# Three of eight contraction tiles of layer 2 as fp32r products of halves, in a four-layer kernel on one core

## The chip, the cores and the metric

The kernel runs on one core of one Trainium2 chip. The metric is the device time of one execution in microseconds. Each core has five engines with an instruction queue each, which work off their queues in order and meet at semaphores: TensorE (PE, matrix products, with weight loads shown apart as PEld), VectorE (DVE), ScalarE (ACT), GpSimd (POOL) and SyncE (SP). Here SP issues the loads and stores, and GpSimd issues transfers that add to what lies in SBUF.

## The reference

Eight batches of 256 rows and 1024 columns in fp32 go through four layers, each with a residual:

```python
x = x + (x @ W0.T + (x @ A0[label]) @ B0.T * 0.5)           # layer 0, low rank 32
x = x + quantise(x, thresholds, deltas, zero_points)        # layer 1, eight groups
x = x + x @ W2[adapter].T                                   # layer 2, weights by batch
x = x + (x @ B3[adapter].T) @ A3[adapter].T                 # layer 3, rank 16
```

In layer 1 the group of an element is the number of thresholds that its magnitude does not exceed; it is rounded with the step and zero point of its group (the last group's for eight), clipped to levels 0 to 63 and scaled back, and is zero where it exceeds none of the thresholds. The kernel works out a candidate for each of the eight groups, and masks choose among them.

## The kernel before, in words

**Layout.** x is held transposed: 128 partitions by eight tiles of 256 rows each (2048 columns for a batch). Each matrix product has 128x128 weights and 128x256 data. An output tile `o` of layer 0 or 2 sums eight contraction tiles `k`.

**Layer 0** (`main0`, `close0`, in order by `tile0`) works with fp32r halves: w0 and x are split once into a high and a low half, and a product becomes three (high by high, high by low, low by high; L773). From batch 2 on the low half of x is made so: ACT copies x into `x_hi` (L369), writes its negative into `x_lo` (L374), and GpSimd issues a transfer that adds `x_raw` to it (L340). A low-rank part (L799, L806) closes each tile (L783).

**Layer 1** runs on ACT and DVE in units (`quantise(u)`): for batch 0 two halves, for batches 1 to 6 one unit of 2048 columns each, for batch 7 three pieces. For each of eight groups ACT makes a candidate (L439) and from the second on a mask (L449); DVE scales (L608), clips (L616) and merges (L628, L634). There are three candidate buffers and two masks, so candidate j+2 and test j+1 wait for merge j-1. At the end DVE adds the result to x2 (L685). `between(u, j)` puts the other work of ACT and DVE between the groups: ACT's splits and drains (`split_batch`, `split_a3`, `drain_low`, `drain_l0`, `drain_bx`, `split_bx`), and DVE's `drain_l2`, `split_a3`, `low_rank_lo` and `split_bx`. `drain_l0` (L400) moves a half of layer 0 from PSUM to x2; from batch 2 on it waits until x3 of the batch two before is complete, since that reads the same slot.

**Layer 2** (`layer2(b, q)`, L838) works in fp32, in four quarters of two output tiles. Two PSUM banks alternate, so quarter 2 waits for DVE's drain of quarter 0 (L595, `x3_done`) and quarter 3 for that of quarter 1. The weights come in 1 MB chunks of two tiles, three chunks deep (`w2_sb`). Batch 7 goes another way (`last_layer2`, L853), by parts of k.

**Layer 3** multiplies x3 with B3 (`low_rank3`, L872), has ACT copy it to `bx_parts` (L412), sums the pieces on PE (`sum_bx`, L879), splits (L421 on ACT, L587 on DVE), multiplies with A3 (L902) and has DVE add it (`finish`, L600); then SP stores.

**PE's order.** In step s = 1 to 6 PE does the four quarters of layer 2 of batch s-1, with the low-rank product and sum of batch s+2 before quarters 2 and 3, then seven tiles of layer 0 (`AHEAD`); behind the third of these comes `low_rank3` of batch s-1, behind the fourth `sum_bx`, behind the fifth layer 3. DVE and ACT work at the same time on unit s. The layer 0 tile with o = 0 needs the bank that ACT's `drain_l0` of the batch before has emptied. In step 1 that tile is the third of the seven, in step 2 the fourth.

## Time and profile before

| | us |
|---|---|
| median of 3 runs | 464.55 |
| lowest, highest | 464.13, 465.97 |
| the profiled execution | 464.56 |
| its span, first to last instruction | 462.7 |
| busy: PE, DVE, ACT, GpSimd | 454.7, 415.4, 326.7, 8.1 |

The span is 1.86 us shorter than the time of the same execution. Busy times are those of the whole span; they do not tell which engine sets the end of a step, since an engine can have idle time that lies in one place only. The granted clock of TensorE was 0.998 of full over the span.

### The profile page before, as it was taken

Reading aid. Unit: us, or ns where it says so; the run is one execution under the profiler, and the core shown is the slowest. Engines: PE = TensorE matmul, PEld = TensorE weight load, DVE = VectorE, ACT = ScalarE, POOL = GpSimd, SP = SyncE. Lnnn points to the kernel's source line nnn. Section 1 sums busy time; section 2 is a strip of 40 time slices with the busy share of each in tenths; the row PEclk is TensorE's granted clock in tenths of the full one; section 3 lists DMA queues with packets and bytes.
Section 4 is the critical chain, followed back from the end, with each engine's and each line's share of the span. In section 5 each row is a group of like instructions: output and inputs, shape, how many; then the busy total and the mean of one; then the engine's idle time right before and its main releaser. Section 6 shows DMA issues by size and latency. Waiting matters only on the chain.

```text
span 462.7 us, 7306 instructions
## 1 busy us (share of the span) xinstructions
PE 454.7 (98%) x3006; PEld 410.9 (89%) x3006; DVE 415.4 (90%) x395; ACT 326.7 (71%) x274; POOL 8.1 (2%) x18
## 2 busy tenths in 40 slices
PE   7999999999999999999999999999999999999995
PEld 7899999889998899889998899989998899988884
DVE  4889999999699996999699996999869999999983
ACT  5699979958398747967398754996349848665730
POOL 1000000000000000000000000100000000000000
PEclk9999999999999999999999999999999999999999
DMA  7983430557128534367227543183322522245242
GB/s 279 343 334 104 91 103 1 91 188 279 69 92 221 196 142 159 69 204 279 76 91 188 197 174 126 48 261 132 120 92 91 181 92 96 75 173 180 94 159 91
DMA packets 17941, 69.15 MB, mean 149 GB/s; under 512 B 2421, under 2 KB 3445, under 8 KB 13045
## 3 DMA queue, kind: packets, MB, share of 16 engines
q1 hardware_dynamic: 17044, 62.41, 37.5%
q0 software_dynamic: 864, 6.29, 7.3%
q8 instruction: 23, 0.38, 0.3%
q14 instruction: 10, 0.07, 0.1%
HBM read 54.01 MB, written 8.39 MB: 135 GB/s over the span
## 4 chain that ended last, share of the span: by engine, by line
PE 90%; DMA 3%; issue 2%; DVE 2%; SPq 2%; ACT 1%; DVEq 0%; ACTq 0%
PE l_ps L838 39%; PE l_ps L773 37%; PE l_ps L853 6%; PE bx_ps L872 2%; PE l_ps L783 2%; DMA w_sb<-w 2%; PE bx_ps L799 2%; DMA adapter_ids<-adapters 1%; PE l_ps L902 1%; PE bx_ps L806 1%; PE bx_ps L879 1%; DVE quant L628 1%; ACT cand L439 0%; ACT magnitude L429 0%; SPq L287 0%
## 5 line engine op out<-in xcount | busy, mean ns | idle before, releaser
L838 PE MATMUL l_ps<-x,w_sb 128*128 128x256 f32 x896 | 196.9, 380 | 0.4 <-DVE x L595 0.4
L838 PEld LDWEIGHTS l_ps<-x,w_sb 128*128 128x128 f32 x896 | 169.2, 190 | 25.3 <-issue 2.8
L634 DVE COPY_PREDICATED quant<-mask,cand 128x2048 f32<-128x2048 int8 (+2 forms) x77 | 145.6, 1891 | 0.4
L439 ACT ACTIVATE cand<-x,inv_delta 128x2048 f32<-128x2048 f32 (+2 forms) x88 | 134.5, 1528 | 8.8 <-DVE quant L628 7.0
L449 ACT ACTIVATE mask<-magnitude,thr_bias 128x2048 fp8e5<-128x2048 f32 (+2 forms) x77 | 117.7, 1529 | 13.4 <-DVE quant L634 12.7
L608 DVE TENSOR_SCALAR cand<-cand,delta 128x2048 f32<-128x2048 f32 (+2 forms) x88 | 87.9, 999 | 10.1 <-ACT cand L439 9.8
L616 DVE TENSOR_SCALAR cand<-cand,lower,upper 128x2048 f32<-128x2048 f32 (+2 forms) x88 | 93.4, 1062 | 0.4
L773 PE MATMUL l_ps<-x_hi,w_hi 128*128 128x256 f32 x512 | 87.1, 292 | 0.9 <-DVE x_lo L565 0.9
L773 PE MATMUL l_ps<-x_hi,w_lo 128*128 128x256 f32 x512 | 82.8, 283 | 0.0
L773 PE MATMUL l_ps<-x_lo,w_hi 128*128 128x256 f32 x512 | 82.5, 283 | 0.0
L773 PEld LDWEIGHTS l_ps<-x_hi,w_hi 128*128 128x128 f32 x512 | 71.4, 191 | 6.6 <-issue 4.2
L773 PEld LDWEIGHTS l_ps<-x_hi,w_lo 128*128 128x128 f32 x512 | 70.7, 192 | 0.2 <-DVE w_lo L559 0.2
L773 PEld LDWEIGHTS l_ps<-x_lo,w_hi 128*128 128x128 f32 x512 | 70.6, 191 | 0.0
L400 ACT ACTIVATE x<-l_ps 128x1024 f32<-128x1024 f32 x16 | 16.3, 1020 | 26.3 <-PE l_ps L783 18.1
L595 DVE TENSOR_TENSOR x<-l_ps,x 128x512 f32<-128x512 f32 x32 | 22.5, 704 | 3.4 <-PE l_ps L853 1.8
L853 PE MATMUL l_ps<-x,w_sb 128*128 128x256 f32 x96 | 21.6, 381 | 0.0
L421 ACT ACTIVATE bx_split<-bx_ps 128x256 fp32r<-128x256 f32 x8 | 3.1, 383 | 25.3 <-PE bx_ps L879 17.4
L853 PEld LDWEIGHTS l_ps<-x,w_sb 128*128 128x128 f32 x96 | 18.1, 190 | 2.9 <-issue 0.4
L628 DVE SCALAR_TENSOR_TENSOR quant<-magnitude,sorted_thr,cand 128x2048 f32<-128x2048 f32 (+2 forms) x11 | 19.4, 1764 | 0.0
L685 DVE TENSOR_TENSOR x<-x,quant 128x2048 f32<-128x2048 f32 (+2 forms) x11 | 18.8, 1708 | 0.1
L587 DVE SCALAR_TENSOR_TENSOR bx_split<-bx_split,not_bx_hi,bx_ps 128x256 fp32r<-128x256 f32 x8 | 3.8, 481 | 16.7 <-ACT bx_split L421 16.7
L600 DVE TENSOR_TENSOR x<-l_ps,x 128x512 f32<-128x512 f32 x24 | 15.1, 688 | 3.7 <-PE l_ps L902 3.1
(66 smaller groups left out, 231.0 us busy)
## 6 DMA issues: line engine op xcount, KB each, us to landing
w_sb<-w SPq DMA_DIRECT2D x31, 1024.0 KB, 4.9
out<-x SPq DMA_DIRECT2D x32, 256.0 KB, 2.2
x_raw<-x SPq DMA_DIRECT2D x15, 512.0 KB, 6.4
x_lo<-x_raw POOLq DMA_DIRECT2D x6, 1024.0 KB, 8.2
a_raw<-a SPq DMA_DIRECT2D x8, 512.0 KB, 3.6
w_sb<-w SPq DMA_DIRECT2D x7, 512.0 KB, 7.4
b_sb<-b SPq DMA_DIRECT2D x8, 256.0 KB, 2.7
a_raw<-a SPq DMA_DIRECT2D x8, 128.0 KB, 6.3
```

Of the source, the lines that this page charges most:

```text
L400: act.activation(x2[:, b % SLOTS, h * HW:(h + 1) * HW], l0_ps[:, h, :], ACT.Copy).then_inc(x0_done, 1)
L439: act.activation(cand[:, c % CANDS, 0:n], x2_unit(u), ACT.Identity, bias=ROUND, scale=inv_delta[:, k:k + 1]).then_inc(rounded, 1)
L449: act.activation(mask[:, m % MASKS, 0:n], magnitude[:, 0:n], ACT.Relu, bias=thr_bias[:, k:k + 1], scale=STEEP, saturate=False).then_inc(ma ...
L595: dve.tensor_tensor(x3[:, cols], l2_bank(b, q), x2[:, b % SLOTS, cols], ALU.add).then_inc(x3_done, 1)
L608: dve.tensor_scalar(t, t, -ROUND, delta[:, k:k + 1], ALU.add, ALU.mult).then_inc(scaled, 1)
L616: dve.tensor_scalar(t, t, lower[:, k:k + 1], upper[:, k:k + 1], ALU.max, ALU.min).then_inc(clipped, 1)
L628: dve.scalar_tensor_tensor(y, magnitude[:, 0:n], sorted_thr[:, G - 1:G], t, ALU.is_gt, ALU.mult)\
L634: dve.copy_predicated(y, mask[:, m % MASKS, 0:n].bitcast(I8), t).then_inc(merged, 1)
L685: dve.tensor_tensor(x2_unit(u), x2_unit(u), quant[:, 0:UNITS[u][2]], ALU.add).then_inc(x2_done, 1)
L773: nc.tensor.matmul(dst, w[:, o, k * P:(k + 1) * P], v[:, b % 2, k * S:(k + 1) * S], start=(o % 2 == 0 and v is x_hi and w is w0_hi and k = ...
L838: last = nc.tensor.matmul(l2_bank(b, q)[:, i * S:(i + 1) * S], w2_tile(b, o)[:, k * P:(k + 1) * P], x2[:, b % SLOTS, k * S:(k + 1) * S], s ...
L853: last = nc.tensor.matmul(l2_bank(b, q)[:, i * S:(i + 1) * S], w2_tile(b, o)[:, k * P:(k + 1) * P], x2[:, b % SLOTS, k * S:(k + 1) * S], s ...
```

## The change

For batches 0 to 6, contraction tiles 0 to 2 (`EDGE = 3`) of layer 2 are now computed like layer 0, as three fp32r products of halves; tiles 3 to 7 stay fp32. In each quarter the fp32 products of both output tiles come first, then the fp32r ones. Batch 7 stays fp32 throughout.

- **Weights.** Layer 2's weights are loaded tile by tile, in two parts: 640 columns into a ring of five (`w2_sb`), and 384 columns, the "edge", into a ring of three (`w2_edge`). ACT copies an edge to `w2_hi` and writes its negative to `w2_lo` (rings of four), and GpSimd issues a transfer that adds the edge to `w2_lo`.
- **x2.** ACT copies the first 768 columns of x2 of the finished batch to `x2_hi`, and DVE subtracts to get `x2_lo`.
- **Room.** To fit into SBUF, w0 is staged in the candidate buffers, `a3_raw` lies in the second half of x3 (so it is loaded behind the stores), one `parts` serves for `low_parts` and `bx_parts`, B3 is held at half the width, and batch 7's last tiles go to freed buffers.

The core of the diff:

```diff
-CHUNKS = 3
+
+EDGE = 3
+SPLIT = B - 1
+EW = EDGE * P
+EX = EDGE * S
+
+RING = 5
+RAW = 3
+HALVES = 4
...
-        w2_sb = sb("w2_sb", [P, CHUNKS, 2, T * P], F32)
+        w2_sb = sb("w2_sb", [P, RING, T * P - EW], F32)
+        w2_edge = sb("w2_edge", [P, RAW, EW], F32)
+        w2_hi = sb("w2_hi", [P, HALVES, EW], F32R)
+        w2_lo = sb("w2_lo", [P, HALVES, EW], F32R)
+        x2_hi = sb("x2_hi", [P, EX], F32R)
+        x2_lo = sb("x2_lo", [P, EX], F32R)
...
+        def hi_tile(b, o):
+            return w2_hi[:, (T * b + o) % HALVES, :]
+
+        def lo_tile(b, o):
+            return w2_lo[:, (T * b + o) % HALVES, :]
+
+        def a3_raw(b):
+            return x3[:, HW:BW] if b < B - 1 else quant[:, HW:BW]
...
+            def load_w2(b, o, adapter):
+                n = T * b + o
+                if b == B - 1 and o >= RING:
+                    sp.wait_ge(x2_done, LAST)
+                elif n >= RING:
+                    sp.wait_ge(w2_used, n - RING + 1)
+                sp.dma_start(w2_tile(b, o), w2[bass.ds(adapter, 1), o, :, EW:T * P].rearrange("l p w -> p (l w)"))\
+                  .then_inc(w2_loaded[o] if b < B - 1 else last_w2_loaded[o], 16)
...
+                elif n >= RAW:
+                    sp.wait_ge(w2_added[(n - RAW) % T], 16 * ((n - RAW) // T + 1))
+                sp.dma_start(edge_tile(b, o), w2[bass.ds(adapter, 1), o, :, 0:EW].rearrange("l p w -> p (l w)"))\
+                  .then_inc(w2_edge_loaded[o] if b < B - 1 else last_w2_loaded[o], 16)
...
+            for o in range(RAW, T - 1):
+                load_edge(0, o, adapter)
+            for s in range(1, B):
...
+                for o in range(RING, T):
+                    load_w2(s - 1, o, adapter)
+                load_edge(s - 1, T - 1, adapter)
+                adapter = adapter_of(s)
+                if s < B - 1:
+                    for o in range(RING):
+                        load_w2(s, o, adapter)
+                        if o == 1 and s + 3 < B:
                             load_batch(s + 3)
-                    if s == B - 1:
-                        load_w2(s, 3, adapter)
-                    load_adapter(s, adapter)
-                for q in range(4) if s < B else LAST_ORDER:
+                        if o < RAW:
+                            load_edge(s, o, adapter)
+                    for o in range(RAW, T - 1):
+                        load_edge(s, o, adapter)
+                else:
+                    for o in range(RING):
+                        load_edge(s, o, adapter)
...
+                load_b3(s, adapter)
+                for q in range(4):
                     store(s - 1, q)
+                if s < B - 1:
+                    load_a3(s, adapter)
...
-            for b in range(ADDED, B):
-                add_x(b)
+            def add_w2(b, o):
+                pool.wait_ge(w2_neg_done, T * b + o + 1)
+                pool.dma_start(lo_tile(b, o), edge_tile(b, o), accum_op=ALU.add).then_inc(w2_added[o], 16)
+
+            add_x(2)
+            for o in range(HALVES):
+                add_w2(0, o)
+            for s in range(1, B):
+                if s + 2 < B:
+                    add_x(s + 2)
+                for o in range(HALVES, T):
+                    add_w2(s - 1, o)
+                if s < SPLIT:
+                    for o in range(HALVES):
+                        add_w2(s, o)
...
+            def split_w2(b, o):
+                n = T * b + o
+                act.wait_ge(w2_edge_loaded[o], (b + 1) * 16)
+                if n >= HALVES:
+                    act.wait_ge(l2_done, n - HALVES + 1)
+                act.activation(hi_tile(b, o), edge_tile(b, o), ACT.Copy).then_inc(w2_hi_done, 1)
+                act.wait_ge(w2_hi_done, n + 1)
+                act.activation(lo_tile(b, o), hi_tile(b, o).bitcast(F32), ACT.Copy, scale=-1.0).then_inc(w2_neg_done, 1)
+
+            def split_x2(b):
+                act.wait_ge(x2_done, x2_count(b))
+                if b > 0:
+                    act.wait_ge(l2_done, T * b)
+                act.activation(x2_hi[:, :], x2[:, b % SLOTS, 0:EX], ACT.Copy).then_inc(x2_hi_done, 1)
...
+                    if j >= 4:
+                        split_w2(0, j - 4)
                 elif s < B - 1:
-                    if j == 1 and s + 2 < B:
-                        split_batch(s + 2)
+                    if j == 1:
+                        split_x2(s - 1)
+                        if s + 2 < B:
+                            split_batch(s + 2)
+                    if j == 2:
+                        split_w2(s - 1, 4)
+                        split_w2(s - 1, 5)
                     if j == 3:
                         split_a3(s - 1)
                         if s + 2 < B:
                             drain_low(s + 2)
-                    if j == 4 and s + 2 < B:
-                        low_rank_hi(s + 2)
+                    if j == 4:
+                        split_w2(s - 1, 7)
+                        if s + 2 < B:
+                            low_rank_hi(s + 2)
+                    if j == 5 and s < SPLIT:
+                        split_w2(s, 0)
+                        split_w2(s, 1)
                     if j == 6:
                         drain_l0(s + 1, 0)
+                        if s < SPLIT:
+                            split_w2(s, 2)
+                            split_w2(s, 3)
...
                 elif u == LAST:
+                    if j == 1:
+                        split_x2(s - 1)
                     if j == 2:
                         split_a3(s - 1)
                     if j == 3:
                         drain_l0(s, 1)
+                    if j >= 4:
+                        split_w2(s - 1, j)
...
+                    if j == 4 and 0 < UNITS[u][0] < B - 1:
+
+                        split_w2(UNITS[u][0] - 1, 6)
...
+            def split_x2(b):
+                dve.wait_ge(x2_hi_done, b + 1)
+                dve.tensor_tensor(x2_lo[:, :], x2[:, b % SLOTS, 0:EX], x2_hi[:, :].bitcast(F32),
+                                  ALU.subtract).then_inc(x2_split_done, 1)
...
                     for q in range(4):
                         finish(UNITS[u][0] - 1, q)
+                if UNITS[u][0] < SPLIT and u > 0:
+                    split_x2(UNITS[u][0])
...
             def layer2(b, q):
-                pe.wait_ge(w2_loaded[q], (b + 1) * 16)
                 if q == 0:
                     pe.wait_ge(x2_done, x2_count(b))
                     if b > 0:
                         pe.wait_ge(out_done, 4 * b - 1)
-                else:
-                    if q > 1:
-                        pe.wait_ge(x3_done, b * 4 + q - 1)
+                elif q > 1:
+                    pe.wait_ge(x3_done, b * 4 + q - 1)
+
                 for i in range(2):
                     o = 2 * q + i
-                    for k in range(T):
-                        last = nc.tensor.matmul(l2_bank(b, q)[:, i * S:(i + 1) * S], w2_tile(b, o)[:, k * P:(k + 1) * P],
-                                                x2[:, b % SLOTS, k * S:(k + 1) * S], start=(k == 0), stop=(k == T - 1))
-                last.then_inc(l2_done, 1)
+                    pe.wait_ge(w2_loaded[o], (b + 1) * 16)
+                    for k in range(EDGE, T):
+                        last = nc.tensor.matmul(l2_bank(b, q)[:, i * S:(i + 1) * S], w2_block(b, o, k),
+                                                x2[:, b % SLOTS, k * S:(k + 1) * S], start=(i == 0 and k == EDGE),
+                                                stop=False)
+                    last.then_inc(w2_used, 1)
+                if q == 0:
+                    pe.wait_ge(x2_split_done, b + 1)
+                for i in range(2):
+                    o = 2 * q + i
+                    pe.wait_ge(w2_added[o], 16 * (b + 1))
+                    hi = hi_tile(b, o)
+                    lo = lo_tile(b, o)
+                    for w, v in ((hi, x2_hi), (hi, x2_lo), (lo, x2_hi)):
+                        for k in range(EDGE):
+                            last = nc.tensor.matmul(l2_bank(b, q)[:, i * S:(i + 1) * S], w[:, k * P:(k + 1) * P],
+                                                    v[:, k * S:(k + 1) * S], start=False,
+                                                    stop=(i == 1 and w is lo and k == EDGE - 1))
+                    last.then_inc(l2_done, 1)
```

**How the order moves.** The names are those of the tiles without their numbers: `x<-l_ps` on ACT is `drain_l0`, `w_hi<-w_edge` with `w_lo<-w_hi` a `split_w2`, `x_hi<-x` of 128x768 ACT's `split_x2`. Line numbers of the changed kernel differ from those of the kernel before.

DVE, from the last merge of unit 1 to the first merge of unit 2. Before:

```order
L634 COPY_PREDICATED quant<-mask,cand 128x2048 [waits merged,masked,clipped]
L587 SCALAR_TENSOR_TENSOR bx_split<-bx_split,not_bx_hi,bx_ps 128x256 [waits bx_hi_done]
L685 TENSOR_TENSOR x<-x,quant 128x2048 [waits merged]
L600 TENSOR_TENSOR x<-l_ps,x 128x512 [waits l3_done] x3
L600 TENSOR_TENSOR x<-bx_ps,x 128x512 [waits l3_done]
L608 TENSOR_SCALAR cand<-cand,delta 128x2048 [waits rounded]
```

Now:

```order
L781 COPY_PREDICATED quant<-mask,cand 128x2048 [waits merged,masked,clipped]
L729 SCALAR_TENSOR_TENSOR bx_split<-bx_split,marks,bx_ps 128x256 [waits bx_hi_done]
L832 TENSOR_TENSOR x<-x,quant 128x2048 [waits merged]
L742 TENSOR_TENSOR x<-l_ps,x 128x512 [waits l3_done] x3
L742 TENSOR_TENSOR x<-bx_ps,x 128x512 [waits l3_done]
L746 TENSOR_TENSOR x_lo<-x,x_hi 128x768 [waits x2_hi_done]
L755 TENSOR_SCALAR cand<-cand,delta 128x2048 [waits rounded]
```

The subtraction for `x2_lo` of the finished batch now stands between the finishes and the first scaling of the next unit, with a wait for ACT.

ACT, from the split of `bx` at the end of a unit to the split of the next x. Before:

```order
L421 ACTIVATE bx_split<-bx_ps 128x256 [waits l3_done,bx_sum_done]
L400 ACTIVATE x<-l_ps 128x1024 [waits x3_done,l0_done]
L439 ACTIVATE cand<-x,inv_delta 128x2048 [waits merged,x0_done]
L429 ACTIVATE magnitude<-x 128x2048 [waits masked,merged,x0_done]
L439 ACTIVATE cand<-x,inv_delta 128x2048 [waits merged]
L449 ACTIVATE mask<-magnitude,thr_bias 128x2048 [waits merged,mag_done]
L439 ACTIVATE cand<-x,inv_delta 128x2048 [waits merged]
L369 ACTIVATE x_hi<-x_raw 128x1024 [waits l0_done,x_loaded0]
```

Now:

```order
L524 ACTIVATE bx_split<-bx_ps 128x256 [waits l3_done,bx_sum_done]
L502 ACTIVATE x<-l_ps 128x1024 [waits x3_done,l0_done]
L559 ACTIVATE cand<-x,inv_delta 128x2048 [waits merged,x0_done]
L547 ACTIVATE magnitude<-x 128x2048 [waits masked,merged,x0_done]
L559 ACTIVATE cand<-x,inv_delta 128x2048 [waits merged]
L569 ACTIVATE mask<-magnitude,thr_bias 128x2048 [waits merged,mag_done]
L559 ACTIVATE cand<-x,inv_delta 128x2048 [waits merged]
L539 ACTIVATE x_hi<-x 128x768 [waits l2_done,x2_done]
L467 ACTIVATE x_hi<-x_raw 128x1024 [waits l0_done,x_loaded0]
```

The copy to `x2_hi` stands behind three candidates' worth of work of the next unit: candidates 0 to 2, the magnitude and test 1.

ACT, from candidate 7 to the split of `bx`. Before:

```order
L439 ACTIVATE cand<-x,inv_delta 128x2048 [waits merged]
L400 ACTIVATE x<-l_ps 128x1024 [waits x3_done,l0_done]
L449 ACTIVATE mask<-magnitude,thr_bias 128x2048 [waits merged]
L412 ACTIVATE bx_parts<-bx_ps 128x256 [waits bx_sum_done,bx_done]
L421 ACTIVATE bx_split<-bx_ps 128x256 [waits l3_done,bx_sum_done]
```

Now:

```order
L559 ACTIVATE cand<-x,inv_delta 128x2048 [waits merged]
L502 ACTIVATE x<-l_ps 128x1024 [waits x3_done,l0_done]
L531 ACTIVATE w_hi<-w_edge 128x384 [waits l2_done,w2_edge_loaded2]
L533 ACTIVATE w_lo<-w_hi 128x384 [waits w2_hi_done]
L531 ACTIVATE w_hi<-w_edge 128x384 [waits l2_done,w2_edge_loaded3]
L533 ACTIVATE w_lo<-w_hi 128x384 [waits w2_hi_done]
L569 ACTIVATE mask<-magnitude,thr_bias 128x2048 [waits merged]
L515 ACTIVATE parts<-bx_ps 128x256 [waits bx_sum_done,low_sum_done,bx_done]
L524 ACTIVATE bx_split<-bx_ps 128x256 [waits l3_done,bx_sum_done]
```

Four instructions, two weight pairs, now stand between the drain of layer 0, which waits for x3, and the drain of `bx`, for which PE waits.

## Rows read from the trace of the kernel before

**Rows 1.** The page: busy us, share of the span, instructions.

```profile
PE 454.7 (98%) x3006; PEld 410.9 (89%) x3006; DVE 415.4 (90%) x395; ACT 326.7 (71%) x274; POOL 8.1 (2%) x18
```

**Rows 2.** Waits of PE: line waited for, us in total, times, longest.

```profile
PE l_ps L910 <- POOL ident L323: 1.5, 1, 1.5
```

**Rows 3.** Windows, step 2: length, then busy us by engine, clock, DMA share.

```profile
133.60:186.30 52.70, 52.70 (x349) 47.44 (x348) 48.42 (x37) 38.53 (x28) 0.86 (x1) 1.00 0.50 157
```

**Rows 4.** Chain in order of time, step 2: start us, us, what.

```profile
155.97 6.91 PE l_ps L838 x32
162.88 2.87 PE l_ps L773 x24
...
176.05 0.43 PE bx_ps L879 x2
...
186.32 13.82 PE l_ps L838 x64
```

**Rows 5.** DVE's timeline, steps 1 and 2: start, us, instruction [idle before].

```profile
129.63 1.28 DVE L608 TENSOR_SCALAR cand<-cand,delta 128x2048 f32<-128x2048 f32 x1
...
133.40 2.35 DVE L628 SCALAR_TENSOR_TENSOR quant<-magnitude,sorted_thr,cand 128x2048 f32<-128x2048 f32 x1
...
143.51 2.52 DVE L634 COPY_PREDICATED quant<-mask,cand 128x2048 f32<-128x2048 int8 x1
...
147.54 0.69 DVE L595 TENSOR_TENSOR x<-l_ps,x 128x512 f32<-128x512 f32 x1 [0.28 <-PE l_ps L838]
...
165.21 0.69 DVE L595 TENSOR_TENSOR x<-l_ps,x 128x512 f32<-128x512 f32 x1
...
182.34 1.28 DVE L608 TENSOR_SCALAR cand<-cand,delta 128x2048 f32<-128x2048 f32 x1
```

**Rows 6.** ACT's timeline, step 2.

```profile
166.00 1.03 ACT L400 ACTIVATE x<-l_ps 128x1024 f32<-128x1024 f32 x1 [2.02 <-DVE x L595]
...
176.52 0.39 ACT L421 ACTIVATE bx_split<-bx_ps 128x256 fp32r<-128x256 f32 x1 [3.20 <-PE bx_ps L879]
...
187.25 1.99 ACT L369 ACTIVATE x_hi<-x_raw 128x1024 fp32r<-128x1024 f32 x2
```

**Rows 7.** Groups by form: busy, mean ns; neighbours of the new forms.

```profile
L369 ACT ACTIVATE x_hi<-x_raw 128x1024 fp32r<-128x1024 f32 x14 | 14.0, 1044 | 0.0
...
L421 ACT ACTIVATE bx_split<-bx_ps 128x256 fp32r<-128x256 f32 x8 | 3.1, 383 | 25.3 <-PE bx_ps L879 17.4 <-PE bx_ps L872 7.8
...
L565 DVE TENSOR_TENSOR x_lo<-x_raw,x_hi 128x512 fp32r<-128x512 f32 x4 | 2.8, 688 | 3.9 <-ACT x_hi L362 3.9
...
L362 ACT ACTIVATE x_hi<-x_raw 128x512 fp32r<-128x512 f32 x4 | 2.4, 622 | 3.4 <-DMA x_raw<-x 3.4
L571 DVE TENSOR_TENSOR x_lo<-x_raw,x_hi 128x1024 fp32r<-128x1024 f32 x2 | 2.4, 1232 | 0.0
```

**Rows 8.** DMA issues: KB each, median us to landing.

```profile
out<-x SPq DMA_DIRECT2D x32, 256.0 KB, 2.2
...
x_lo<-x_raw POOLq DMA_DIRECT2D x6, 1024.0 KB, 8.2
```

**Rows 9.** ACT's timeline, step 1.

```profile
81.50 1.99 ACT L369 ACTIVATE x_hi<-x_raw 128x1024 fp32r<-128x1024 f32 x2
```

**Rows 10.** Waits of ACT from 239.00 to 291.70 us.

```profile
ACT x L400 <- PE l_ps L783: 2.6, 1, 2.6
```

**Rows 11.** ACT's timeline, unit 6.

```profile
341.48 1.02 ACT L400 ACTIVATE x<-l_ps 128x1024 f32<-128x1024 f32 x1 [6.46 <-PE l_ps L783]
...
351.93 1.99 ACT L449 ACTIVATE mask<-magnitude,thr_bias 128x2048 fp8e5<-128x2048 f32 x1
```

**Rows 12.** DVE's timeline: first merge of unit 6, last x2 addition.

```profile
349.47 2.34 DVE L628 SCALAR_TENSOR_TENSOR quant<-magnitude,sorted_thr,cand 128x2048 f32<-128x2048 f32 x1
...
444.38 0.68 DVE L685 TENSOR_TENSOR x<-x,quant 128x512 f32<-128x512 f32 x1
```

**Rows 13.** PE's timeline: its last part of layer 2.

```profile
446.73 5.45 PE L853 MATMUL l_ps<-x,w_sb 128*128 128x256 f32 x24
```

## What I predict

> **What bounds the kernel now.** First the page: TensorE (PE) is busy 98% of the span [rows 1]. Then the waits with PE as the waiting engine: the longest is 1.5 us, before its first product, and no other of the four lines reaches 1 us [rows 2]. Then one steady step in the windows: in 52.70 us PE is busy 52.70, VectorE (DVE) 48.42, ScalarE (ACT) 38.53, at the full granted clock [rows 3]. So PE is the bound, but DVE has only 4.3 us of slack in a step. The chain in order of time shows PE's step as a grid [rows 4]: a quarter of layer 2 takes 6.91 us, a tile of layer 0 (24 fp32r products and a short one) 3.00 us.
>
> The reader should then put DVE's and ACT's timelines of this step beside the grid [rows 5, 6]. ACT reaches batch s-1's `bx` work early, waits for PE's sum (ends 176.48), splits `bx`, drains layer 0, and only then starts the candidates of the next batch. DVE, its merges done, waits there too, then adds (L685), finishes (L600) and opens the next batch's unit with L608 at 182.34, 5.86 us after PE's sum.
>
> **The change part by part.**
>
> PE: a fp32 product takes 13.82 us / 32 = 0.432 us, a fp32r one 2.87 us / 24 = 0.120 us [rows 4]. Three of the latter save 0.072 us; 3 x 8 x 7 = 168 of them save **12.1 us**, 1.73 us in a step. The page shows no cost for changing between the kinds: a layer 0 tile behind layer 2 takes 2.87 us. The Trainium skill (FP8 and Floating Point Precision, TensorE Precision Notes) says that true fp32 makes four passes. As an estimate from that page, at one pass for fp32r, three products would cost three quarters of one, and 168 x 0.108 = 18.1 us would be saved; the row says 0.83 of one, and the row decides.
>
> DVE: one subtraction of 128x768 (`x2_lo`) for each of seven batches. Its neighbours are 0.688 us (128x512) and 1.232 us (128x1024) [rows 7]; I take 0.95. With it DVE has 49.4 us of work in a step.
>
> ACT: a conversion of 128x768 per batch (between 0.622 and 1.044 us [rows 7], taken as 0.83), and for each of 56 weight tiles a copy and a negation of 128x384, of which the second waits for the first. One lies between 0.383 and 0.622 us [rows 7]; a pair is bounded by 0.8 and 1.3, taken as 1.02. In a step 8 x 1.02 + 0.83 = 9.0 us on top of 38.53: 47.5 us, which fits by itself. ACT's waits in the step are 14 us.
>
> GpSimd and the queues: 56 adding transfers of 192 KB. The nearest rows are the 1 MB adding transfer (8.2 us to landing) and the 256 KB store (2.2 us) [rows 8]; I take 4.5, nearer to the store by size but with descriptors from GpSimd. The Trainium skill (DMA: Bandwidth & Descriptors, Anatomy of one DMA — SWDGE (gpsimd) path) gives 2.0 us plus bytes over 436 GB/s: an estimate of 2.5 us here, and 4.4 for the 1 MB one, where the trace has 8.2. By either figure up to 5.0 us the sum below is the same. On SP the stores of batch s-1 now stand behind `edge` loads that wait for these adds, but the last of those adds lands by the end of the unit, before the first store may go; `a3`, loaded behind the stores, has ten microseconds in hand. I cost these at nothing; w2's tiles are asked for a quarter or more ahead.
>
> **What is not hidden is the order.** DVE's new subtraction of batch b stands before the first L608 of unit b+1, and waits for `x2_hi`, which ACT makes only after five full operations of unit b+1. Before, ACT's same place is the first L369, at 187.25: 10.77 us behind PE's sum at 176.48 [rows 4, 6]. So with t for the end of PE's sum and d for the time at which DVE may start a unit: d = t + 10.77 + 0.83 + 0.95 = **t + 12.55**, where it was t + 5.86. DVE starts each unit 6.7 us later against PE, more than its slack. What is late next, from offsets in the same unit (start 129.63; merge 2 at 143.51) [rows 5]:
> - x3's quarter 3 is ready at d + 36.0 (165.21 + 0.69 is 36.3, less a wait of 0.28 at 147.54). ACT's drain of layer 0 waits for that; behind it in ACT's queue now stand two weight pairs, a test and the `bx` drain that PE's sum needs: 0.1 + 0.95 + 2.05 + 1.9 + 0.45, and the sum itself with its signals 0.5: **t' = d + 42.0**.
> - Tile 7's low half: merge 2 ends at d + 16.4; a test, a pair, a candidate and a pair on ACT give d + 22.3; with 4.5 for the add, 1.08 of products and 13.60 to the sum: d + 41.5.
> So a step is 42.0 + 12.55 = 54.55 us instead of 52.70; PE's gain of 1.73 us turns into waits.
>
> Now step by step, t before being 123.78, 176.48, 229.19, 281.89, 334.60 (176.48 from [rows 4]; the others are the same sum in the other steps):
> - Start: ACT's first full unit reaches L369 at 81.50 [rows 9]. Four weight pairs stand before it; the first fits into a wait of ACT for PE, three delay it by 3.1. d = 81.5 + 3.1 + 0.83 + 0.95 = 86.4.
> - Step 1: here the layer 0 tile that needs the drained bank stands before the low-rank work of batch 0. x3 complete 86.4 + 36.0, bank free 1.1 later, then 3.00 + 1.00 + 3.18 + 0.43 on PE and 0.1 of signals: t = 131.2 (+7.4).
> - Steps 2 to 4: 54.55 each: 185.8, 240.3, 294.9.
> - Step 5: ACT's second drain of layer 0 waits 2.6 us for PE [rows 10]. Before, this went into slack; now it moves d: t = 352.0 (+17.4).
> - Unit 6 depends on PE's last tile of batch 6: ACT's drain starts 6.88 us behind the sum (341.48) and the place of `x2_hi` comes 10.45 us later (351.93) [rows 11]: d = 352.0 + 6.88 + 10.45 + 0.83 + 0.95 = 371.1. Before, DVE's first merge of this unit began at 349.47 [rows 12]; less 3.77 (129.63 to 133.40 [rows 5]) that is a start at 345.7. DVE is 25.4 us late.
> - From there to its last x2 addition (ends 445.07 [rows 12]) DVE had hardly a gap; one more subtraction adds 0.95. PE then began its last part at 446.73, 1.66 behind [rows 13]. The end moves by 25.4 + 0.95 - 1.66 = 24.7 us. PE's own path (last layer 2 of the steps from 423, then 48.9 us) comes out level with this, at 472.
> The profiled execution took 464.56 us, 1.86 over its span and equal to the median of 464.55. **Forecast: 464.6 + 24.7 = 489 us**.
>
> **The rivals.**
> 1. PE stays the bound: 464.6 - 12.1 = **452.5 us**. (By the Trainium skill's estimate of 18.1 us, FP8 and Floating Point Precision again, this would be 446.5.) This needs `x2_hi` to be done when DVE finishes, at t + 5.9, so ACT would have to be 5.7 us further ahead. ACT's idle time in the step speaks for it; that the idle time lies before the `bx` work and not behind it [rows 6] speaks against it. It decides for the faster side only if that order is not as I read it.
> 2. The adding transfers are slow: at the 8.2 us of [rows 8] tile 7 sets t' = d + 45.2, 3.2 us more in four steps and 0.4 in the first: **502 us**. It decides from a landing of 5.0 us. For it: ten times as many of them, beside more and smaller loads; against it: a fifth of the size.
> 3. Milder: ACT's weight pairs hide and a step stays at about 52.7, the start and unit 6 remaining: 7.4 less in four steps, **482 us**; with half of the start hidden too, 478.
> 4. The gain and the late start cancel (within 0.5% of 464.6): it would take a shift of 6.7 us that costs just 12 us over the kernel; nothing in the rows points there.
>
> **How the numbers follow.** My forecast 0.60, rival 2 0.16, rival 3 0.14, rival 1 0.06, rival 4 0.04. The pair's bounds (0.8 to 1.3) move the forecast by -2 to +2.5 us, the 128x768 forms by 1.3 either way; so its own range is 484 to 494. The range goes down to rival 3's lower figure with its own margin and up past rival 2: 476 to 508. A measurement of this kernel tells about 0.5% from no change: faster 0.06, same 0.04, slower 0.90.
>
> **What would show it.** DVE's largest wait would be its `x2_lo` subtraction (L746) for ACT's `x2_hi` (L539), 4.6 us in the middle steps, more at both ends, some 40 us in all. A step from one layer 2 to the next would be near 54.5 us; a quarter of layer 2 without waits 6.48 us. PE's busy share would fall to some 91%, with new waits for x3 (L737), for ACT's drain and for its `parts`; ACT's L502 would wait for L737. Wrong would be: steps of 51 us, or L539 done before L742; a long wait of L1000 for the adds would mean rival 2.

## The result: slower by 7.4%

| | before | after |
|---|---|---|
| median, us | 464.54 | 499.02 |
| lowest, highest | 463.6, 466.0 | 497.43, 500.81 |
| profiled execution, its span | 464.56, 462.7 | 500.81, 499.0 |
| busy PE, DVE, ACT, GpSimd | 454.7, 415.4, 326.7, 8.1 | 452.9, 420.9, 384.6, 71.7 |

The ratio is 1.0737 (95% interval 1.0686 to 1.0788): 34.5 us more. The forecast was 489.0 us with a range from 476 to 508 and a chance of 0.90 for slower. The direction and the range held; the size was 10 us short.

The page of the changed kernel answers to [rows 1]; then the shares of the chain by engine, and the landing of the new adds, beside [rows 8]. The chain is the path of work that ended last, followed back from each wait to what released it (L429 adds, L746 is `x2_lo`, L539 `x2_hi`, L531 and L533 the weight pair):

```profile
PE 452.9 (91%) x3174; PEld 413.4 (83%) x3174; DVE 420.9 (84%) x402; ACT 384.6 (77%) x393; POOL 71.7 (14%) x74
...
PE 40%; DVE 19%; issue 15%; ACT 13%; DMA 10%; SPq 2%; DVEq 0%; ACTq 0%
...
w_lo<-w_edge POOLq DMA_DIRECT2D x56, 192.0 KB, 4.1
```

PE has not become the one engine of the chain again: its busy time is nearly what it was and its share has fallen to 91%, as forecast. It fell by only 1.8 us instead of 12.1; some 7 us of the missing 10.3 are products that ran at a lower granted clock (last section), the rest isn't placed. The waits that answer to [rows 2] (engine, line, what it waited for; total us, times, longest):

```profile
PE l_ps L1000 <- DMA w_lo<-w_edge: 13.8, 7, 2.9
PE l_ps L987 <- DVE x L737: 12.4, 6, 3.0
PE l_ps L1000 <- DVE x_lo L746: 7.3, 3, 5.0
...
DVE x_lo L746 <- ACT x_hi L539: 43.8, 6, 11.6
...
ACT x L502 <- DVE x L737: 10.7, 5, 4.0
```

DVE waits 43.8 us for `x2_hi`; before, it had no such operation. The chain of step 2 answers to [rows 4] (start, us, what):

```profile
132.15 0.45 PE bx_ps L1042 x2
...
143.44 0.74 ACT x_hi L539
...
144.21 0.96 DVE x_lo L746
...
161.64 1.89 issue
163.53 0.52 ACT w_hi L531
164.06 0.53 ACT w_lo L533
...
164.99 5.95 DMA w_lo<-w_edge
...
170.98 2.41 PE l_ps L1000 x18
...
186.56 0.63 PE bx_ps L1042 x2
```

From PE's sum the chain goes to ACT, which reaches `x2_hi` after 10.8 us; then DVE subtracts and opens its unit at 145.16; from DVE's third merge it goes over a test and a weight pair of ACT, an adding transfer of 5.95 us, 18 products and four tiles of layer 0 (with `low_rank3` before the last) to the end of the next sum, at 187.19. A step is 54.6 us here.

### The profile page after: what moved, and what is told of

Its sections match the earlier page's. It is cut to its first block, busy times and chain, and to the rows that moved or that the text cites. A ratio compares the mean times of both kernels' runs of the same rounds, so it can differ in the third digit from the quotient of the medians.

```text
span 499.0 us, 8182 instructions
## 1 busy us (share of the span) xinstructions
PE 452.9 (91%) x3174; PEld 413.4 (83%) x3174; DVE 420.9 (84%) x402; ACT 384.6 (77%) x393; POOL 71.7 (14%) x74
## 4 chain that ended last, share of the span: by engine, by line
PE 40%; DVE 19%; issue 15%; ACT 13%; DMA 10%; SPq 2%; DVEq 0%; ACTq 0%
PE l_ps L922 25%; DVE cand L755 7%; DMA w_lo<-w_edge 6%; PE l_ps L1016 5%; DVE quant L781 5%; ACT cand L559 4%; ACT mask L569 3%; PE l_ps L1000 3%; DVE quant L775 3%; PE l_ps L987 3%; ACT magnitude L547 2%; DMA cand<-w 2%; PE bx_ps L1035 2%; DMA w_sb<-w 2%; DVE x L737 1%
## 5 line engine op out<-in xcount | busy, mean ns | idle before, releaser
L987 PE MATMUL l_ps<-x,w_sb 128*128 128x256 f32 x560 | 126.7, 381 | 12.4 <-DVE x L737 12.4
L987 PEld LDWEIGHTS l_ps<-x,w_sb 128*128 128x128 f32 x560 | 105.2, 191 | 28.6 <-DVE x L737 15.0
L429 POOL DMA_DIRECT2D w_lo<-w_edge x56 | 64.7, 1168 | 240.3 <-ACT w_lo L533 239.0
L922 PE MATMUL l_ps<-x_hi,w_hi 128*128 128x256 f32 x512 | 87.2, 292 | 3.8 <-ACT x L502 2.4
L922 PE MATMUL l_ps<-x_hi,w_lo 128*128 128x256 f32 x512 | 83.7, 286 | 0.0
L922 PE MATMUL l_ps<-x_lo,w_hi 128*128 128x256 f32 x512 | 83.5, 285 | 0.0
L922 PEld LDWEIGHTS l_ps<-x_hi,w_hi 128*128 128x128 f32 x512 | 72.1, 194 | 9.6 <-issue 3.7
L922 PEld LDWEIGHTS l_ps<-x_lo,w_hi 128*128 128x128 f32 x512 | 71.7, 194 | 0.0
L1000 PE MATMUL l_ps<-x_hi,w_hi 128*128 128x256 f32 x168 | 35.3, 320 | 21.1 <-DMA w_lo<-w_edge 13.8
L1000 PEld LDWEIGHTS l_ps<-x_hi,w_hi 128*128 128x128 f32 x168 | 26.2, 197 | 26.1 <-DMA w_lo<-w_edge 16.5
L746 DVE TENSOR_TENSOR x_lo<-x,x_hi 128x768 fp32r<-128x768 f32 x7 | 6.7, 959 | 43.8 <-ACT x_hi L539 43.8
L502 ACT ACTIVATE x<-l_ps 128x1024 f32<-128x1024 f32 x16 | 16.3, 1018 | 27.7 <-PE l_ps L932 17.0
L531 ACT ACTIVATE w_hi<-w_edge 128x384 fp32r<-128x384 f32 x56 | 28.6, 510 | 8.8 <-DMA w_edge<-w 8.8
L533 ACT ACTIVATE w_lo<-w_hi 128x384 fp32r<-128x384 f32 x56 | 29.4, 525 | 1.8
L1000 PE MATMUL l_ps<-x_hi,w_lo 128*128 128x256 f32 x168 | 30.5, 292 | 0.0
L1000 PE MATMUL l_ps<-x_lo,w_hi 128*128 128x256 f32 x168 | 30.4, 292 | 0.0
```

The source lines that it names most:

```text
L429: pool.dma_start(lo_tile(b, o), edge_tile(b, o), accum_op=ALU.add).then_inc(w2_added[o], 16)
L531: act.activation(hi_tile(b, o), edge_tile(b, o), ACT.Copy).then_inc(w2_hi_done, 1)
L533: act.activation(lo_tile(b, o), hi_tile(b, o).bitcast(F32), ACT.Copy, scale=-1.0).then_inc(w2_neg_done, 1)
L922: nc.tensor.matmul(dst, w[:, o, k * P:(k + 1) * P], v[:, b % 2, k * S:(k + 1) * S], start=(o % 2 == 0 and v is x_hi and w is w0_hi and k = ...
L987: last = nc.tensor.matmul(l2_bank(b, q)[:, i * S:(i + 1) * S], w2_block(b, o, k), x2[:, b % SLOTS, k * S:(k + 1) * S], start=(i == 0 and k ...
L1000: last = nc.tensor.matmul(l2_bank(b, q)[:, i * S:(i + 1) * S], w[:, k * P:(k + 1) * P], v[:, k * S:(k + 1) * S], start=False, stop=(i == 1 ...
```

## Experiments

Each ratio is to runs of the kernel before taken beside it. The theory after the result was this: one loop holds the step, PE's sum, ACT's `x2_hi`, DVE's unit, and back to the sum. The rivals were that the adding transfers, or ACT's and PE's own added work, do it.

### x2_hi early

```diff
                 candidate(u, 0)
+                if 0 < UNITS[u][0] and UNITS[u][1] == 0:
+                    split_x2(UNITS[u][0] - 1)
                 take_magnitude(u)
...
                     if j == 1:
-                        split_x2(s - 1)
```

> The changed kernel with one edit: ACT makes x2_hi of the finished batch right behind candidate 0 of the next unit, not behind candidate 2. Theory A (the place of x2_hi in ACT's queue holds DVE up, by 43.8 us in all): x2_hi is ready 4.1 us behind PE's bx sum instead of 11.6, before DVE has finished, so DVE's wait goes to under 3 us in the middle steps; a step falls from about 55 us to PE's own 51.0. DVE then ends some 7 us earlier than in the kernel before: 457 us (455 to 462). Theory B (the adding transfers, 13.8 us of PE's waits, set the steps whatever DVE does): over 485 us. Theory C (the added work of ACT is too much, wherever it stands): over 480 us.

Measured: 487.07 us (486.51 to 491.74), ratio 1.0485 (1.0467 to 1.0502). That is 12.0 us less than the changed kernel, not 42. Of the 43.8 us of the wait that it was to remove 6.6 are left, 4.8 of them in unit 6, and another wait has grown (the two waits, then the chain of the step from 188 on):

```profile
DVE x_lo L744 <- ACT x_hi L539: 6.6, 3, 4.8
...
PE l_ps L998 <- DMA w_lo<-w_edge: 22.1, 9, 4.4
...
188.16 1.03 ACT x L502
...
216.30 0.54 ACT w_lo L533
...
217.23 8.54 DMA w_lo<-w_edge
...
225.81 3.73 PE l_ps L998 x18
...
242.88 0.45 PE bx_ps L1040 x2
```

Between 188.16 and 216.84 ACT runs with no wait for another engine; every step of the chain is its own. So there is a **second loop**: from PE's sum through all that stands in ACT's queue up to the pair of tile 6 (28.7 us), its add, and PE's tiles back to the sum, 55.5 us in this step. In the changed kernel it lay hidden beside the first: with the landing of 5.95 us and the 2.41 us of products of its step 2 it would be 51.6 us, as an estimate. Here the landing took 8.54 us and the 18 products 3.73, at a granted clock of 0.58.

The steps of this kernel are therefore no shorter. The ends of its sums lie 57.5, 55.5, 57.4 and 54.9 us apart, against 54.6, 56.9, 54.8 and 57.2, and in step 5 the two kernels are level (the changed one first):

```profile
355.48 0.60 PE L1042 MATMUL bx_ps<-parts,bx_sum 128*128 128x256 f32 x2
...
354.98 0.60 PE L1040 MATMUL bx_ps<-parts,bx_sum 128*128 128x256 f32 x2
```

The spans of these two executions differ by 9.1 us (499.0 and 489.9; this execution was the slowest of the kernel). All but 0.5 of it was gained behind step 5.

The landings are longer here. SP asks for a batch of x (1 MB) just ahead of this add (in step 2 the changed kernel, then this one):

```profile
161.77 0.84 SPq L262 DMA_DIRECT2D x_raw<-x  x2
...
158.69 0.84 SPq L262 DMA_DIRECT2D x_raw<-x  x2
...
159.76 9.36 DMA w_lo<-w_edge
```

In the changed kernel the add of tile 6 starts 3.2 to 3.4 us behind that request in steps 2 to 4 and takes 5.95, 7.01 and 6.31 us; here it starts 0.7 to 1.4 us behind it and takes 9.36, 8.54 and 9.51. From the request to the landing it is 9.2 to 10.4 us in all six cases. In the kernels "`x2_lo` late", "the load of x later" and "the splits earlier" the add in the chain behind the request (tile 6 or 7) lands 8.8 to 10.7 us behind it, in the same three steps of each. In step 5, for which SP asks for no batch, no add from 315 to 356 takes more than 5.6 us in any of the five kernels. So the long landings go with the request for x, and behind it an add that starts earlier hardly lands earlier.

### x2_lo late

```diff
                         clip(u, j + 1)
+                    if j == 0 and 0 < UNITS[u][0] and UNITS[u][1] == 0:
+                        split_x2(UNITS[u][0] - 1)
                     between(u, j)
```

> The changed kernel with ACT's order untouched, but DVE subtracts for x2_lo behind merge 0 of the next unit instead of ahead of its first scaling. Theory A: DVE goes on 5.9 us behind the bx sum as in the kernel before and reaches the subtraction at 13.2, when x2_hi (11.6) is ready; x2_lo is then ready at 14.1, just as PE comes to its fp32r products (14.2). 459 us (455 to 466). Theory B or C: over 480 us. If only ACT's queue mattered and not that DVE stands waiting, this edit would change nothing (499).

Measured: 487.44 us (485.55 to 489.24), ratio 1.0511 (1.0489 to 1.0532). Cutting the first loop at another point gives the same time as the kernel above, and the miss is the same. The chain shows what held it, an add, then a load of an edge. ACT waits for that load 5.0 us, and from there the chain goes over its queue and two merges of DVE to ACT's drain at 237.59:

```profile
212.57 8.57 DMA w_lo<-w_edge
...
221.29 3.77 DMA w_edge<-w
```

So ACT's queue with the weight tiles is under both kernels, though the two edits touch different engines. An add that an edge load waits for is more than the second loop: it is the ring that comes up again below.

### No adding transfers

```diff
-                    pe.wait_ge(w2_added[o], 16 * (b + 1))
+                    pe.wait_ge(w2_neg_done, T * b + o + 1)
```

The 56 adds are left out, and SP's load of an edge waits for ACT's negation too.

> The changed kernel without the 56 adding transfers of layer 2's weights: PE and the edge ring wait for ACT's negation instead. Left out of the computation: the weight itself in the low halves, which stay the negated high halves. Theory A: the path over ACT (x3, drain of layer 0, two weight pairs, test 7, bx) is nearly as long as that over the adds (both about 42 us from the start of DVE's unit), so a step only loses up to 1.5 us and the moments of lower clock behind the longest waits: 490 us (486 to 495). Theory B: the steps fall to 51 to 52 us and the time to 475 or less.

Measured: 494.8 us (493.37 to 495.62), ratio 1.0662 (1.0644 to 1.068). The transfers alone are worth 4.2 us, since the first loop stays: DVE's wait for `x2_hi` is still 42.8 us.

### Three fp32 products for nine fp32r ones

```diff
-                    for w, v in ((hi, x2_hi), (hi, x2_lo), (lo, x2_hi)):
...
+                                                hi[:, k * P:(k + 1) * P].bitcast(F32),
+                                                x2[:, b % SLOTS, k * S:(k + 1) * S], start=False,
```

> The changed kernel with the nine fp32r products of each tile replaced by three fp32 products of w2_hi and x2, with all waits, splits and adds kept. Left out of the computation: the low halves of these weights. PE has 12.1 us more work than in the changed kernel. Theory A (PE no longer sets the steps): only what stands behind the last wait of a step shows, two tiles at 0.22 us each in six steps, and the last layer 2, 1.7 us: 503 us (501 to 506). If PE still set the steps: 511 us.

Measured: 502.23 us (499.79 to 504.36), ratio 1.0799 (1.0765 to 1.0833). PE's saving of 12.1 us, undone with all the rest kept, reaches the end with 3.2 us (the interval overlaps that of the changed kernel), far from the 12.1 of a kernel that PE sets.

### Both loops cut

This and the next three kernels build on `x2_hi` early. The first of them joins the two edits "x2_hi early" and "no adding transfers".

> x2_hi early and no adding transfers for the weights, both edits at once (low halves of the weights stay the negated high halves). Alone they gave 487.1 and 494.8 us, 12 and 4 less than the changed kernel. Theory A2: two loops of nearly equal length hold the step, one over DVE's late unit and one over ACT's queue, tile 6's split and its add (28.9 us on ACT from the bx sum to the negation, 6.0 to 8.5 us for the add, 2.2 to 3.7 us of products, 13.6 us to the next sum: 51 to 55 us); each hides the other, so both edits together give much more than 16 us: PE's own 51.0 us a step, 458 us (454 to 463). Theory B2: the effects add up, as with two independent delays: 483 us. Theory C (too much ACT work): not below 475 us.

Measured: 466.3 us (465.16 to 466.93), ratio 1.0041 (1.0021 to 1.0062). One edit gave 12.0 us and the other 4.2; together they give 32.7. Two loops of nearly equal length side by side do that, additive costs don't. The chain is now PE's own over whole steps (the first products of layer 2 in two steps):

```profile
188.65 4.32 PE l_ps L972 x20
...
239.61 4.32 PE l_ps L972 x20
```

A step is 239.61 - 188.65 = 50.96 us, and the next is the same (290.57): the 52.70 of [rows 3] less the 1.73 that the prediction had worked out. Yet the kernel isn't faster than the one before. Four rows tell why, the first of step 1, the others of unit 6:

```profile
118.48 4.63 PE l_ps L907 x24
...
357.11 6.27 PE l_ps L972 x20
...
381.04 1.02 ACT L489 ACTIVATE x<-l_ps 128x1024 f32<-128x1024 f32 x1 [4.82 <-PE l_ps L917]
...
385.99 2.56 DVE L766 COPY_PREDICATED quant<-mask,cand 128x2048 f32<-128x2048 int8 x1 [1.52 <-ACT mask L556]
```

In step 1 PE waits 3.9 us for ACT's drain, whose unit had started later behind the first weight pairs, and the 24 products behind the wait take 4.63 us instead of 2.88. Its step 2 begins at 188.65 - 50.96 = 137.69, where it was 133.62: 4.1 us of loss. Four steps give back 6.3. The step of unit 6 loses again: there `x2_hi` stands behind a drain that waits for PE's last tile, DVE waits 4.14 us for it, PE then waits 2.02 us for x3, and the 20 records behind that take 6.27 us instead of 4.32; so the sum of this step starts at 386.22, where it was 385.71. At the end of the unit ACT waits 4.82 us for PE's last tile, makes two weight pairs behind that, and only then DVE's last mask. DVE's closing addition of unit 6 (L817) begins at 388.83; before, it began at 388.63. From there DVE works nearly without a gap to its last addition of x2, at 445.47 (before 444.38, [rows 12]), and the chain from 385.99 to 439.60 is DVE's; then it goes over ACT's `parts` copy to PE's sum at 441.28, and PE's last part follows at 447.83 (before 446.80). So the end belongs to the end of unit 6 and DVE's work on batch 7. It nearly did so before: PE's last part stood only 1.66 us behind the addition that it needs, and at the tighter place, the `parts` copy (ended 440.12) in front of PE's sum (440.52), the lead was 0.4 us. Here PE waits 1.89 us for that copy.

### The load of x later

```diff
-                        if o == 1 and s + 3 < B:
-                            load_batch(s + 3)
                         if o < RAW:
                             load_edge(s, o, adapter)
+                        if o == 2 and s + 3 < B:
+                            load_batch(s + 3)
```

> x2_hi early, and SP issues the next batch's x load (1 MB) behind the edge load that waits for tile 7's add, not two tiles earlier; nothing left out. Theory A2 with contention: the add of tile 6 took 8.5 us because the x load was issued 1.4 us ahead of it; now it lands in 4 to 5 us, a step is 28.9 + 4.5 + 2.2 + 13.6 = 49.2 us by that loop, so PE's 51.0 sets it: 459 us (455 to 466). Rival (the landing is long because of the weight loads and the small rows, not of x): adds of 6.5 us or more, steps of 52 to 53 us, 470 to 480 us. If the place of the adds did not matter: 487 us.

Measured: 481.45 us (477.18 to 484.34), ratio 1.0386 (1.0332 to 1.0439), 5.6 us less than `x2_hi` early alone. Both ranges are missed; the rival's 470 to 480 is nearest. PE's wait for the adds falls from 22.1 to 7.8 us, but the chain of step 3 now goes over the add of tile 7, which lands in 8.83 us behind the load of x, the edge load behind it, for which ACT waits 3.55 us, and a test: DVE waits 18.2 us for masks (5.0 with `x2_hi` early alone), PE 6.4 us for `parts` (1.0). ACT's waits for an edge are 14.7 us in all, 4 times; they were 19.9, 4 times.

### The splits of tiles 6 and 7 earlier

```diff
                         split_w2(s - 1, 4)
                         split_w2(s - 1, 5)
+                        split_w2(s - 1, 6)
...
                             drain_low(s + 2)
-                    if j == 4:
                         split_w2(s - 1, 7)
...
-                    if j == 4 and 0 < UNITS[u][0] < B - 1:
-                        split_w2(UNITS[u][0] - 1, 6)
```

> x2_hi early, and ACT splits tile 6 right behind tile 5 and tile 7 behind the bx drain one group earlier; the x load stays where it was. Theory A2: tile 6's negation is ready at about 22.5 us behind the bx sum instead of 28.9, so its add lands before PE needs it (34.6); tile 7's edge is loaded only behind tile 4's add, its negation at about 28 to 30, its add with the x load beside it at 37, 1 to 2 us late: a step of 51 to 52.5 us, 463 us (458 to 470). If ACT's order before the add did not matter (contention alone): 480 us or more.

Measured: 485.81 us (483.93 to 486.03), ratio 1.0448 (1.0413 to 1.0482). The interval overlaps that of `x2_hi` early alone. An earlier place for the pairs is worth nothing by itself that can be told from noise. PE's wait for the adds falls from 22.1 to 15.9 us; ACT now waits for an edge 8 times (10.3 us in all) instead of 4 (19.9), and DVE still 12.0 us for ACT's `bx_split` (12.1). Which of these eats the gain wasn't traced.

### All three moves

> x2_hi early, splits of tiles 6 and 7 earlier, x load later; nothing left out. Theory A2: every loop but PE's own is now shorter than 51.0 us, so PE sets the steps: 457 us (454 to 461), faster than the kernel before by 1 to 2%. If the added transfers and ACT work cost anything by themselves beyond their places, it stays above 465 us.

Measured: 480.01 us (478.77 to 481.69), ratio 1.0325 (1.0295 to 1.0355). The number forecast was missed by 23 us. The chain shows a **third loop**, a ring through the edge buffers:

```profile
203.76 5.78 DMA w_lo<-w_edge
...
209.68 2.29 DMA w_edge<-w
...
212.00 0.54 ACT w_hi L531
...
222.30 7.05 DMA w_lo<-w_edge
...
229.51 2.43 DMA w_edge<-w
...
231.96 0.53 ACT w_hi L531
```

There are three edge buffers. In the changed kernel itself SP's queue already waits 43 times for an add before it can ask for an edge:

```profile
SPq L295 <- DMA w_lo<-w_edge: 190.3, 43, 9.3
```

SP may load one only when the add of three tiles before has landed, and ACT's copy, which stands ahead of tests and candidates in ACT's queue, waits for that load. So ACT pays for an add and a load in turn (8.2 and 9.7 us here), though PE waits only 0.4 us for adds in this stretch (190 to 250).

### All three moves, no adding transfers

> The kernel with x2_hi early, the x batch's load behind edge 2 and tiles 6 and 7 split one and two groups earlier (480.01 us with the adding transfers), now also without those transfers of the weights, so that the low halves are minus the high ones and the result of layer 2 is wrong by the low parts. Theory ring: what holds that kernel at 480 is a ring over the edge buffers: add, then SP's edge load, which waits for the add of three tiles before, then ScalarE's copy, which waits for the load and stands in ScalarE's queue ahead of the tests. Without the adds an edge buffer is free as soon as ScalarE has negated the copy, so the ring loses the add's 6 to 7 us and the time falls to 458 to 464 us, at or under the 466.3 us of the kernel with x2_hi early and no adds. Rival queue: ScalarE's own queue (47.5 us of work in a step of 51) sets 480 whatever the adds do: 474 to 480 us.

Measured: 468.79 us (467.12 to 469.73), ratio 1.0096 (1.0072 to 1.0121). This lies between the theory's 458 to 464 and the rival's 474 to 480. The transfers are worth 11.2 us here. The middle steps are PE's again, with the same 50.96 us (layer 2 from 189.84 to 240.80).

The theory failed in its absolute number for the reasons seen above: step 1 (layer 2 of step 2 begins at 138.88 instead of 133.62), and the end, where PE waits 1.99 us for the `parts` copy. The two moves cost 2.5 us where no transfer is there to hide.

### All three moves, adds from DRAM

```diff
-                    sp.wait_ge(w2_added[(n - RAW) % T], 16 * ((n - RAW) // T + 1))
+                    sp.wait_ge(w2_hi_done, n - RAW + 1)
...
-                pool.dma_start(lo_tile(b, o), edge_tile(b, o), accum_op=ALU.add).then_inc(w2_added[o], 16)
+                pool.dma_start(lo_tile(b, o), w2[0:1, o, :, 0:EW].rearrange("l p w -> p (l w)"), accum_op=ALU.add)\
+                    .then_inc(w2_added[o], 16)
```

> The same three moves, with as many adding transfers of the same 192 KB, but their source is matrix 0 of layer 2's weights in DRAM and no longer the edge buffer, so that the load of an edge waits for ScalarE's copy of the tile three before and not for its add (the data added is that of another matrix for most batches, so the low halves are wrong there). TensorE still waits for every add. Theory ring: what counts is that ScalarE is tied to the adds by the edge buffers; untied, the time falls from 480 to 464 to 470 us, with waits of ScalarE for w_edge near none (12.1 us in the kernel with the buffers tied). Rival product: what counts is TensorE's own wait for the low halves and the load that the transfers put on the queues: 476 to 482 us, no change.

Measured: 473.58 us (473.12 to 474.11), ratio 1.019 (1.0168 to 1.0212). The same number of transfers of the same size, but ACT is untied from them: 6.4 us less than with the edge buffers tied, and ACT has no wait for an edge in its list. Without transfers at all it was 4.8 us less again. So of the 11.2 us the ring is over half, if the source costs nothing by itself; it may cost something, since these adds land in 5.5 us in the median, the others in 4.6. What is left goes with PE's wait for the adds:

```profile
201.32 8.96 DMA w_lo<-w
...
PE l_ps L996 <- DMA w_lo<-w: 10.0, 9, 3.0
```

Each theory of the expectation named one part, and both parts are there.

### x2_hi early, adds from DRAM

> The kernel with only x2_hi early (487.07 us), with the adds read from DRAM and the edge buffers released by ScalarE's copy, as in the run beside it. There TensorE waited 22.1 us for the adds and only then for anything else, and the chain of waits went over ScalarE's own queue up to the pair of tile 6 and its add of 8.5 us beside the loads of x. Theory ring: the ties of ScalarE to the adds are little of this one, since the chain held no wait of ScalarE for an edge: 480 to 487 us. Rival: the whole of the difference to 464 is the ring: 464 to 470 us.

Measured: 484.26 us (480.64 to 487.16), ratio 1.0422 (1.0356 to 1.0488). Against 487.07 that is little, as the theory said, and the intervals overlap: here the second loop holds, and its chain had no wait for an edge. PE still waits 16.7 us for adds. So with only `x2_hi` early the ring hardly counts, though ACT waited 19.9 us for edges there; it counts in the kernels whose chains show it.

## Why the prediction was right or wrong

**The bound and the first loop: right, and measured to a tenth.** From PE's sum to the start of DVE's unit t + 12.55 was forecast. The chain gives 145.16 - 132.60 = 12.56, 199.76 - 187.19 = 12.57 and 256.69 - 244.12 = 12.57; in the fourth step, where ACT's second drain waits for PE, 15.3 (forecast 15.15). The single costs: `x2_lo` 0.958 (0.95), `x2_hi` 0.827 (0.83), a weight pair 0.508 + 0.525 = 1.03 (1.02). A quarter of layer 2 without waits took 4.32 + 2.15 = 6.47 us (6.48), as the row shows:

```profile
430.64 4.32 PE l_ps L987 x20
434.96 2.15 PE l_ps L1000 x18
```

So a product of 256 columns takes 0.432 us in fp32 (two records of 0.216) and 0.120 in fp32r; and three of these cost 0.83 of one of those, as [rows 4] had it. The estimate of three quarters, worked out from the four passes of the Trainium skill (FP8 and Floating Point Precision, TensorE Precision Notes) and an assumed one pass for fp32r, does not agree with this trace: the ratio of the two products is 3.6.

**The way back to the sum: right size, wrong path in part.** d + 42.0 was forecast, over x3 and ACT's drain. Measured: 42.0, 44.4, 42.2, 41.9. But in the first three of these steps the chain goes over the add of tile 6, which the prediction didn't look at (it took tile 7, which is the chain in the fourth): with its start 19.8 us behind DVE's and 16.3 from landing to sum, this path is 36.1 us plus the landing. At the forecast 4.5 us it wouldn't have counted; with 5.95 it is as long as ACT's path. The term that was mis-sized is the landing: the chain has 5.95, 7.01, 6.31 and 4.27 us, though the median of all 56 is 4.1. The adds that matter lie in the stretch in which SP asks for weights and x as well, and land some 9 to 10 us behind the request for x (first experiment). A median was the wrong number to forecast. Rival 2 (from a landing of 5.0 us on) is thereby true in part; in step 3 it cost 2.4 us, together with the clock (below).

**Step by step** (end of PE's sum): forecast 131.2, 185.8, 240.3, 294.9, 352.0; measured 132.6, 187.2, 244.1, 298.9, 356.1. Of the 4.1 us that are missing there, 1.4 came in step 1 and 2.4 in step 3, in both with a stretch at a lower granted clock:

```profile
123.20:127.90 4.70, 4.65 (x29) 4.42 (x32) 4.54 (x4) 3.77 (x6) 2.42 (x2) 0.64 0.47 102
226.50:230.60 4.10, 4.01 (x21) 4.01 (x22) 4.04 (x5) 1.21 (x3) 1.51 (x1) 0.58 0.71 185
404.40:408.80 4.40, 4.40 (x27) 4.40 (x26) 4.40 (x4) 2.61 (x2) 1.74 (x1) 0.61 1.04 246
```

(The window, its length, busy time and count of PE, PEld, DVE, ACT and GpSimd, then the granted clock, the DMA share and GB/s.) The mean clock of 0.6 says that most of the stretch ran at the lower level of 1.2 GHz. The prediction had no term for that.

**Unit 6 and the end: two terms missing.** DVE's start in unit 6 was 375.2 (forecast 371.1, the same 4.1). The prediction then said that DVE has hardly a gap; it waited 4.7 us for its last mask:

```profile
414.93 1.02 ACT L502 ACTIVATE x<-l_ps 128x1024 f32<-128x1024 f32 x1 [7.92 <-PE l_ps L932]
...
417.80 1.99 ACT L569 ACTIVATE mask<-magnitude,thr_bias 128x2048 fp8e5<-128x2048 f32 x1
...
419.87 2.58 DVE L781 COPY_PREDICATED quant<-mask,cand 128x2048 f32<-128x2048 int8 x1 [4.70 <-ACT mask L569]
```

ACT's drain stands before the mask of test 7, with two weight pairs (1.95 us) between them, and waits for PE, which was itself late by an add (a wait of 2.88 us) and its lower clock (4.37 us for 24 products). PE's last steps of layer 2 began at 430.64 instead of about 423, and took 51.9 us to the last part, not 48.9: of those 3.0 us more, 1.5 are one more wait for an add, 0.5 a wait for a tile of batch 7, and 1.0 isn't placed. The last part, before at 446.80 [rows 13], begins at 482.55. The end moved by 36.3 us in the profiled execution, where 24.7 was forecast. The difference on PE's path: 4.1 up to step 5, 3.5 in step 6, 3.0 in the last stretch, in sum 10.6, on top of the 25.2 at which PE's own path had been forecast (472 against 446.80); the last part itself took 0.5 us longer. The median lies 1.8 us under that execution.

**Rival 1 (452.5 us) was wrong as a number, not only unlikely.** The prediction said that it needs just `x2_hi` done early. The first kernel of the experiments did that and came to 487. Behind the first loop lay a second, and a third behind that. Even without the adds and with steps of 50.96 us the kernel took 466: in it PE's saving didn't reach the end. Whether another order of the work in step 1 and unit 6 would let it through wasn't tried. What was missing from the sum "464.6 - 12.1" is the end: it took PE's share of 98% for the whole path, while DVE was only 1.66 us from being late at the last part, which is in the prediction's own rows [rows 12, 13], and ACT's `parts` copy 0.4 us from being late at the sum before.

**What stays open.** Why the same transfer lands in 2.9 us at one time and 7.9 at another is only placed, not explained: the long ones of the chains land a nearly fixed time behind the request for x, and are missing in the step without one, and the run with that request two tiles later cut PE's waits to a third. By what the two transfers hinder each other isn't shown. What the two moves of loads and splits cost in the kernel without transfers (2.5 us) wasn't traced to its term. Four edge buffers weren't tried; the run with adds from DRAM changed the source of the transfer together with the tie.

## What to carry to other kernels

When a change adds work to the engines beside the bound one, follow every loop from the bound engine's result back to its next input, through each in-order queue, with its length; cutting the longest one gains at most the difference to the next, and the next can grow: here the add moved closer to a large load and landed later. Three loops had nearly the step's length, and the proof was in pairs of edits: 12.0 and 4.2 us alone, 32.7 together. A saving on the bound engine counts up to where another engine ends the last unit; look for the other engines' lead at the end (here 0.4 and 1.66 us) before anything is subtracted from the total.

## What the runs showed of the hardware

**The clock after a wait.** Before the change PE had almost no waits and a mean granted clock of 0.998. The changed kernel's waits, by the same line form as [rows 6], and what followed:

```profile
98.97 4.58 PE L987 MATMUL l_ps<-x,w_sb 128*128 128x256 f32 x20 [2.97 <-DVE x L737]
...
123.25 0.74 PE L922 MATMUL l_ps<-x_hi,w_hi 128*128 128x256 f32 x4 [2.39 <-ACT x L502]
...
226.59 0.72 PE L1000 MATMUL l_ps<-x_hi,w_hi 128*128 128x256 f32 x3 [2.49 <-DMA w_lo<-w_edge]
...
327.00 4.58 PE L987 MATMUL l_ps<-x,w_sb 128*128 128x256 f32 x20 [2.87 <-DVE x L737]
...
375.27 1.01 PE L1000 MATMUL l_ps<-x_hi,w_hi 128*128 128x256 f32 x3 [5.03 <-DVE x_lo L746]
...
376.00:380.00 4.00, 4.00 (x19) 3.91 (x18) 3.96 (x4) 0.12 (x1) 0.00 (x0) 0.50 0.00 0
```

Behind the waits of 2.39, 2.49 and 5.03 us the clock fell to its lower level (0.50 in the last window), and behind the one of 2.88 us that ended at 403.08 a little later; 24 products took 4.46 and 4.37 us instead of 2.88, and 18 took 3.92 instead of 2.15. Behind the waits of 2.97 and 2.87 us (rows 98.97 and 327.00) it stayed at full, 1.00 in the 4.5 us that follow, as it did behind eleven shorter ones of 1.07 to 1.99 us. So the length of the wait alone doesn't tell which level follows; what does isn't shown here. Each of the four places with the lower level cost 1.5 to 2.3 us beyond the wait. A change that trades a full PE for one with waits can pay this on top, wherever PE is next on the path.

**Adding transfers.** GpSimd's 192 KB adds landed in 2.9 to 7.9 us in the changed kernel (median 4.1), in up to 9.9 in another (`x2_lo` late), and read from DRAM in 3.6 to 9.1 (median 5.5). GpSimd itself was busy 71.7 us instead of 8.1, 1.2 us in the mean for each issue (0.9 in the median), which nobody waited for here.
